# Residual sums into the tile's other buffer, and the first pair's tiles spread over more groups of the MLP stage

## The chip, the cores and the metric

One Trainium2 chip, one core. The time is the device time of one execution in microseconds (us); the median of three runs of the kernel before is 3148.65 us (3146.72 to 3151.5).

## The reference

For x of 2 x 4096 x 512 (8192 tokens, model width 512), all in float32:

```
xn = layernorm(x)
a  = xn + ssm_scan(rmsnorm(xn, scale1))                # a diagonal state space model over the sequence
h  = gelu(rmsnorm(a, scale2) @ w1 + b1) @ w2 + b2      # 512 -> 2048 -> 512, exact gelu
f  = fp4_linear(silu(fp4_linear(xn, w_gate)) * fp4_linear(xn, w_up), w_down)   # 512 -> 1408 -> 512, blockwise FP4
out = x + (a + h) + f
```

The change touches only how the tiles of `h` are prepared: for each tile of 128 tokens, `a` (called x1), the sum of squares of x1, the normalized rows, and the residual sum `z + b2 + x1`, where z holds x + f.

## The kernel before, in words

The work is cut into 64 tiles of 128 tokens. Every float32 operand of a matmul is split into a high and a low half (fp32r), and a product takes three passes (`PASSES`). Five programs, one per engine, are written out in full; each engine takes its instructions in this written order, and semaphores tie them together. SP (the sync engine) issues all DMAs, in its own order, and waits where its program waits.

Until about 1725 us the kernel computes the FP4 layers of all tiles and the state space scan. r_Z holds x + f per tile, r_Y the scan's result.

Then comes the MLP stage (1725 to 1990 us), with `NB1 = 2` blocks of four tiles, tiles 0 to 7. Its loop is `for n in range(2, 16 * NB1 + 2)` in each program. In group n PE does `mlp1(n)` (first layer, feature block n % 16, twelve matmuls into one bank) and `mlp2(n - 2)` (second layer, twelve). `mlp1(n)` needs the GELU of group n - 2 (its bank is free then), and in the first block the low half of weight set n; `mlp2(n - 2)` needs the split GELU of its group. `mlp1(16)` needs all of tiles 4 to 7. At n = 17 DVE writes block 0's results, and SP stores them. The programs of DVE, ACT and POOL in group n are, in order:
- DVE: `w_low(n + 2)` (low halves of a weight set, while n + 2 < 16), `gelu_parts(n)`, from n = 26 on a turn or low half of the first pair's operands (`conv_turn`, `conv_sums`, `conv_low`), `result` at 17 and 33, then the steps of `mlp_steps(n)`, then those of `early_steps(n)`.
- ACT: `w_high(n + 2)`, `gelu(n)`, the scale of combined weights k (`combine_scale`) and the high half of the k of one group earlier (`combine_high`, one buffer `wh`, which waits for the store of the k before), then the tile steps.
- POOL: `combine_sums`, `combine_low`, then the tile steps.
- SP: the store of the low half, the store of the high half and the load of the combined weights, the tile steps, from n = 18 on one `ring_load` per group, and at n = 29 and 31 `quarters`.

A tile's steps have three parts. Part 0: `tile_add` on DVE (x1 = normalized x + scan result, in `xl`, after the loads of `xl` and `yl`), `tile_square` on ACT (writes its squares to `yl`, which no one reads, and the sum of squares), `tile_z` on POOL (`zl + b2`, then `+ x1`), on SP the load of the next `zl` (tiles below 8). Part 1: `tile_root` on DVE (eleven small steps and the scale of `xl`, which waits for `tile_z`), and on SP the stores and loads that follow. Part 2, tiles 4 to 7 only: DVE turns the tile, ACT writes its high half to `hT`, DVE the low half, and SP issues the loads of the tile after next (`pre_load(t + 2)`), which use the same slot and wait for DVE's turn (`s_hs`). `xl` and `yl` exist twice (slot 0 and slot 1), `zl` once.

`mlp_steps(n)` says in which group each part of tiles 4 to 7 runs (L165); within a group, part 2 stands ahead of 0 and 1. `early_steps(n)` (L197) says so for o = 8 to 15, the tiles of the first pair of blocks; part 1 stands ahead of part 0. For these SP does, in part 1 of o:

```
store_sum(o)      # r_Q <- residual sum, after s_zx1
store_normed(o)   # r_N <- xl, after the scale
z_load(o + 1)
pre_load(o + 2)   # for o = 14 and 15: quarters(0, 0) and quarters(0, 1)
```

`quarters` loads the normalized rows back in quarters for the transposition by `conv_turn`. After the loop come seven pairs of blocks (`unit` and `rest`), with products from combined weights that the ring brings in, and the tiles of the next pair prepared by the same functions, one per unit.

Of the kernel before, what the change touches and what calls it, by code (L numbers as in the profile page):

```python
# [39 lines left out]

NB1 = 2
PAIRS = (NT // 4 - NB1) // 2
OLD = 4 * NB1
# [4 lines left out]
WSC0, WSUM0, WAH0, WAL0, HT0 = 4 * NST, 4 * NST, 3, 4, 11  # L48
RING_0, OQ_0, ZQ_0, WT_0, Q_0, WA_0, WB_0, QO_0 = 32, 16, 8 * NT, 16, 16, 16, 16, 16
QUADS = ((0, 1), (2, 3), (4, 0), (1, 2))  # L50
# [114 lines left out]
def mlp_steps(n):  # L165

    b, f = n // 16, n % 16
    if b + 1 >= NB1:
        return []
    at = [(2, 3, 6), (4, 5, 8), (8, 9, 12), (10, 11, 14)]  # L170
    return [(4 * (b + 1) + j, part) for part in (2, 0, 1) for j in range(4) if at[j][part] == f]
# [25 lines left out]
def early_steps(n):  # L197

    return [(OLD + r, part) for part in (1, 0) for r in range(8) if 14 + 3 * r // 2 + part == n]

# [8 lines left out]
def build(nc, x, A, B, C, Dv, sc1, sc2, w1, b1, w2, b2, wg, wu, wd, cst, out):  # L209
# [15 lines left out]
    with ExitStack() as ctx:  # L225
# [308 lines left out]
        def sync_program(e):  # L534
# [148 lines left out]
            def pre_load(o):  # L683
# [14 lines left out]
                e.dma_start(xl[k][:], xt[t]).then_inc(d_xl[o % 2], 16)  # L698
                if p is not None:
                    e.wait_ge(s_sq, p + 1)  # L700
                for i in range(2):
                    e.dma_start(yl[k][:].rearrange("p (g i k) -> p g i k", i=2, k=16)[:, :, i],
                                bass.AP(r_Y.tensor, (64 * i + t) * P * 16, [[16, P], [P * P * 16, 16], [1, 16]])
                                ).then_inc(d_yl[o % 2], 16)

            def z_load(o):
                if o >= NT:
                    return
                t = tile_of(o)
# [15 lines left out]
            def quarters(c, i):  # L725
# [43 lines left out]
            def ring_load(q):  # L769
                if q >= 56 * PAIRS:  # L770
                    return
                if q < 14:
                    e.wait_ge(s_w1, 17 + q)
                    e.wait_ge(d_wa, WA_0 + 16 * 4)
# [4 lines left out]
            def residual_in(c, i):  # L779
                r = 2 * (i % 4) + i // 4  # L780
                if i % 4 < 2 and 2 * c + i // 4 == 0:
                    e.wait_ge(s_w1, 32)
                elif i % 4 >= 2 and i < 4:
# [161 lines left out]
            for n in range(2, 16 * NB1 + 2):  # L945
# [15 lines left out]
                for o, part in early_steps(n):  # L961
                    if part == 1:
# [5 lines left out]
                        else:  # L968
                            quarters(0, o - OLD - 6)
                if 18 <= n < 32:  # L970
                    ring_load(n - 18)
                if n in (29, 31):
                    quarters(0, (n - 25) // 2)
            pre_load(OLD + 8)
# [297 lines left out]
        def vector_program(e):  # L1272
# [374 lines left out]
            def second_part(c, i):  # L1647
# [9 lines left out]
                elif q == 2:  # L1657
                    e.wait_ge(d_oo[6], 16)
                    e.wait_ge(d_oo[7], 16)
                e.tensor_copy(second_high(q), gelued(half, f)).then_inc(s_gh, 1)  # L1660

            def unit(c, u):
# [8 lines left out]
                if g == 0:  # L1671
                    e.wait_ge(d_oo[4], 16)
                e.tensor_tensor(u2[:], bank[5][:], s1[:], ALU.add).then_inc(s_add, 1)
                e.wait_ge(s_p, 7 * g + 3)
                e.wait_ge(s_add, 5 * g + 1)
                if g == 0:
                    e.wait_ge(d_oo[5], 16)
                e.tensor_tensor(u3[:], bank[6][:], u2[:], ALU.add).then_inc(s_add, 1)  # L1678
# [76 lines left out]
            for n in range(2, 16 * NB1 + 2):  # L1755
# [5 lines left out]
                if n < 16 * NB1:  # L1761
                    gelu_parts(n)
                if n >= 26 and n % 2 == 0:
                    conv_turn(0, n // 2 - 13)
                    conv_sums(0, n // 2 - 13)
                elif n >= 27:
                    conv_low(0, n // 2 - 13)
                if (n - 2) % 16 == 15:
# [11 lines left out]
        def scalar_program(e):  # L1780
# [215 lines left out]
            def conv_high(c, i, x):  # L1996
# [3 lines left out]
                if c == 0 and i == 0 and x == 0:  # L2000
                    e.wait_ge(s_w1, 24)
                    e.wait_ge(d_wa, WA_0 + 16 * 16)
                    for j in range(2):
                        e.wait_ge(d_wb[j], WB_0 + 16 * 8)
                    for j in range(4):
                        e.wait_ge(d_oo[j], 16)
                elif c and i == 0 and x == 0:
# [69 lines left out]
            for n in range(2, 16 * NB1 + 2):  # L2077
# [13 lines left out]
                if n >= 26 and n % 2 == 0:  # L2091
                    for x in range(5):
                        conv_high(0, n // 2 - 13, x)
            for c in range(PAIRS):
# [5 lines left out]
        def gpsimd_program(e):  # L2100
# [92 lines left out]
            def tile_z(t):  # L2193
                b, j = t // 4, t % 4
                zz = zx[b % 2][:, j] if t < OLD else zl[:]
                e.wait_ge(d_zl, 16 * (t + 1))
                if t == 0:
                    e.wait_ge(d_cv[0], 16)
                if t == 4:
                    e.wait_ge(s_dn, NW)  # L2200
# [72 lines left out]
            for n in range(2, 16 * NB1 + 2):  # L2273
# [9 lines left out]
                if n >= 27 and n % 2:  # L2283
                    conv_low(0, n // 2 - 13)
            for c in range(PAIRS):
# [65 lines left out]
```

## Time and profile before

| | us |
|---|---|
| median of three runs | 3148.65 |
| the profiled execution | 3141.06 |
| its span | 3139.3 |
| PE busy | 3003.8 (96%) |
| DVE busy | 2186.5 (70%) |
| POOL busy | 1601.4 (51%) |
| ACT busy | 1157.2 (37%) |

A busy share is that of all matmuls; in a row of the timeline the second number is the time from the first start to the last end of the merged instructions, and the bracket holds the idle time of the engine just before, with what ended it. SPq is the queue of DMA issues of SP; an issue's time is not the transfer's. PEclk is the granted clock of TensorE in parts of full speed (2.4 GHz).

### The profile page before, as it was taken

Reading aid. Unit: us, or ns where it says so; the run is one execution under the profiler, and the core shown is the slowest. Engines: PE = TensorE matmul, PEld = TensorE weight load, DVE = VectorE, ACT = ScalarE, POOL = GpSimd, SP = SyncE. Lnnn points to the kernel's source line nnn. Section 1 sums busy time; section 2 is a strip of 40 time slices with the busy share of each in tenths; the row PEclk is TensorE's granted clock in tenths of the full one; section 3 lists DMA queues with packets and bytes.
Section 4 is the critical chain, followed back from the end, with each engine's and each line's share of the span. In section 5 each row is a group of like instructions: output and inputs, shape, how many; then the busy total and the mean of one; then the engine's idle time right before and its main releaser. Section 6 shows DMA issues by size and latency. Waiting matters only on the chain. (4 is left out here: it accounts for less than half of the span.)

```text
span 3139.3 us, 44091 instructions
## 1 busy us (share of the span) xinstructions
PE 3003.8 (96%) x14525; PEld 2417.3 (77%) x14525; DVE 2186.5 (70%) x4455; ACT 1157.2 (37%) x1930; POOL 1601.4 (51%) x1457
## 2 busy tenths in 40 slices
PE   5799999999999999999999877999999999999999
PEld 3678788888877777777777765788888888878887
DVE  8798898987787766767777766656565656565622
ACT  5345655645443443333323432222222222222220
POOL 7556666655555555555454554344454535453413
PEclk9999999999999999999999998999999999999999
DMA  4133334357666666666633788877767677768541
GB/s 127 45 89 96 113 113 117 97 136 188 184 174 168 164 161 175 158 159 167 170 87 94 198 211 200 198 209 174 201 179 209 172 202 182 207 166 215 143 131 47
DMA packets 975794, 488.77 MB, mean 156 GB/s; under 512 B 689232, under 2 KB 817488, under 8 KB 973008
## 3 DMA queue, kind: packets, MB, share of 16 engines
q1 hardware_dynamic: 975568, 485.96, 58.6%
q8 instruction: 118, 1.93, 0.3%
q14 instruction: 108, 0.88, 0.1%
HBM read 346.84 MB, written 138.97 MB: 155 GB/s over the span
## 5 line engine op out<-in xcount | busy, mean ns | idle before, releaser
L1029 PE MATMUL bank<-XT,Wu 128*128 128x512 f32 (+1 forms) x2148 | 515.6, 389 | 15.9 <-DVE sg L1314 15.7
L1029 PE MATMUL bank<-XT,Wg 128*128 128x512 f32 (+1 forms) x2148 | 522.8, 392 | 7.3 <-DVE Wd L1381 7.3
L1051 PE MATMUL bank<-Wd,HT 128*128 128x512 f32 x2112 | 515.6, 393 | 6.6 <-POOL HT L2130 5.3
L2122 POOL TENSOR_TENSOR qa<-qb,qs 128x512 f32<-128x512 f32 (+2 forms) x277 | 308.4, 1114 | 342.5 <-DVE qb L1374 340.1
L1029 PEld LDWEIGHTS bank<-XT,Wu 128*128 128x128 f32 x2148 | 401.0, 190 | 106.6 <-issue 25.7
L1051 PEld LDWEIGHTS bank<-Wd,HT 128*128 128x128 f32 x2112 | 391.7, 188 | 106.1 <-issue 15.4
L1029 PEld LDWEIGHTS bank<-XT,Wg 128*128 128x128 f32 x2148 | 397.3, 189 | 96.0 <-DVE Wd L1381 9.4
L1225 PE MATMUL bank<-Wp,G 128*128 128x512 f32 x1800 | 456.4, 390 | 3.3 <-POOL G L2243 3.3
L1203 PE MATMUL bank<-HC,Wp 128*128 128x512 f32 x1680 | 423.5, 390 | 2.8 <-POOL WH L2236 2.8
L1225 PEld LDWEIGHTS bank<-Wp,G 128*128 128x128 f32 x1800 | 336.7, 188 | 77.4 <-POOL G L2243 7.9
L1203 PEld LDWEIGHTS bank<-HC,Wp 128*128 128x128 f32 x1680 | 316.4, 188 | 69.2 <-POOL WH L2236 3.2
L2130 POOL TENSOR_TENSOR HT<-qb,HT 128x512 fp32r<-128x512 f32 (+1 forms) x179 | 229.9, 1284 | 241.5 <-ACT HT L1816 241.3
L2116 POOL TENSOR_TENSOR qa<-qa,qs 128x512 f32<-128x512 f32 (+1 forms) x243 | 263.0, 1082 | 109.0 <-DVE qs L1354 109.0
L1816 ACT ACTIVATE HT<-qb 128x512 fp32r<-128x512 f32 (+1 forms) x179 | 112.2, 627 | 413.8 <-DVE qb L1328 413.7
L2243 POOL TENSOR_TENSOR G<-gf,G 128x512 fp32r<-128x512 f32 x75 | 103.5, 1379 | 303.6 <-DVE G L1660 303.6
L1225 PE MATMUL bank<-Wp,G2x 128*128 128x512 f32 x888 | 229.0, 390 | 2.0 <-POOL G2x L2243 2.0
L1366 DVE SCALAR_TENSOR_TENSOR qa<-qb,qa 128x512 f32<-128x512 f32 (+2 forms) x149 | 120.7, 810 | 140.9 <-ACT qb L1788 140.6
L1225 PEld LDWEIGHTS bank<-Wp,G2x 128*128 128x128 f32 x888 | 166.1, 188 | 38.5 <-POOL G2x L2243 4.2
L1823 ACT ACTIVATE sg<-bank 128x512 f32<-128x512 f32 (+1 forms) x179 | 105.6, 590 | 203.2 <-PE bank L1029 199.8
L1203 PE MATMUL bank<-WH,Wp 128*128 128x512 f32 x672 | 172.5, 393 | 3.7 <-DVE u L1678 2.4
L1349 DVE TENSOR_REDUCE qs<-qa 128x32 f32<-128x512 f32 (+1 forms) x243 | 165.1, 680 | 8.3
L1328 DVE STREAM_TRANSPOSE qb<-qa 128x512 f32<-128x512 f32 (+1 forms) x179 | 124.9, 698 | 55.6 <-POOL qa L2122 55.6
(199 smaller groups left out, 4420.2 us busy)
## 6 DMA issues: line engine op xcount, KB each, us to landing
Wp<-r_A SPq DMA_DIRECT2D x392, 256.0 KB, 3.3
px<-in_L_attn_x_dram SPq DMA_DIRECT2D x128, 256.0 KB, 3.2
xin<-in_L_attn_x_dram SPq DMA_DIRECT2D x128, 256.0 KB, 3.3
sT<-r_K SPq DMA_DIRECT2D x128, 256.0 KB, 4.1
r_Z<-xin SPq DMA_DIRECT2D x64, 256.0 KB, 2.4
r_U<-ub SPq DMA_DIRECT2D x16, 1024.0 KB, 6.7
sU<-r_U SPq DMA_DIRECT2D x32, 512.0 KB, 4.9
r_Y<-sY SPq DMA_DIRECT2D x16, 1024.0 KB, 5.3
```

Of the source, the lines that this page charges most:

```text
L1029: ins = e.matmul(bk[:, 0:n], W[wh][:, k, :], inputs(xh, w, k), start=(k == 0 and p_ == 0), stop=(k == KD - 1 and p_ == 2))
L1051: ins = e.matmul(DNB[t % 4][:], HT[hh][:, w % 2, a * P:(a + 1) * P], Wd[wh][:, f, :], start=(w == first(n) and p_ == 0), stop=(w == last(n ...
L1203: ins = e.matmul(bank[bk][:], ring(q)[:, 256 * wh_ + P * kt:256 * wh_ + P * kt + P], combined(b, xh)[:, kt], start=(k in OPENS and kt == 0 ...
L1225: ins = e.matmul(bank[4 * half + j][:], (second_high(q), second_low(q))[gh][:, j * P:(j + 1) * P], Wp[f][wh_][:, 1, :], start=(f == 0 and ...
L1328: e.transpose(qb[:, m % 2, 0:n], qa[:, m % 4, 0:n]).then_inc(s_t2, 1)
L1349: e.tensor_reduce(s_, blk(job_in(m)), AX, ALU.max, apply_absolute_value=True).then_inc(s_mx, 1)
L1366: e.scalar_tensor_tensor(Aa, Bb, FLOOR, Aa, ALU.max, ALU.add).then_inc(s_t, 1)
L1816: e.activation(HT[0][:, w % 2, 0:n], qb[:, m % 2, 0:n], ACT.Copy).then_inc(s_hh, 1)
L1823: e.activation(sg[:, 0:n], GB[:, 0:n], ACT.Silu).then_inc(s_sg, 1)
L2116: e.tensor_tensor(blk(qa[:, m % 4, 0:n]), blk(job_in(m)), bc(qs[:, m % 4, 1, 0:n // 16], n // 16), ALU.mult).then_inc(s_pa, 1)
L2122: e.tensor_tensor(blk(qa[:, m % 4, 0:n]), blk(qb[:, m % 2, 0:n]), bc(qs[:, m % 4, 0, 0:n // 16], n // 16), ALU.mult).then_inc(s_ph, 1)
L2130: e.tensor_tensor(lo, qb[:, m % 2, 0:n], hi.bitcast(F32), ALU.subtract).then_inc(s_hl, 1)
```

## The change

`tile_z` writes the residual sum of tiles 8 and up to `yl` of the tile's slot instead of `zl`, once ACT's Square has gone over it; SP stores it from there. So `zl` is free for the next load as soon as POOL has read it (`s_zx1`), and the load of the next `yl` in that slot, and the first two `quarters`, wait for the store of the sum (`d_qo`) instead of the Square. Tiles 6 and 7 run two groups sooner, and the first pair's tiles begin at group 12 rather than 14, one every 7/4 groups instead of 3/2:

| | before | after |
|---|---|---|
| tile 6: parts 0, 1, 2 in group | 8, 9, 12 | 6, 7, 10 |
| tile 7 | 10, 11, 14 | 8, 9, 12 |
| o = 8 to 15, part 0 | 14 15 17 18 20 21 23 24 | 12 13 15 17 19 20 22 24 |
| part 1 | one later each | one later each |

The remaining edits write constants with `LASTB = 16 * (NB1 - 1)` or `OLD`; with `NB1 = 2` they have the same values, and a new wait in `tile_z` for `8 <= t < OLD` is never reached (`OLD` is 8).

```diff
+LASTB = 16 * (NB1 - 1)
...
-    at = [(2, 3, 6), (4, 5, 8), (8, 9, 12), (10, 11, 14)]
+    at = [(2, 3, 6), (4, 5, 8), (8, 9, 12), (10, 11, 14)] if b + 2 < NB1 else [(2, 3, 6), (4, 5, 8), (6, 7, 10), (8, 9, 12)]
...
-    return [(OLD + r, part) for part in (1, 0) for r in range(8) if 14 + 3 * r // 2 + part == n]
+    return [(OLD + r, part) for part in (1, 0) for r in range(8) if LASTB - 4 + 7 * r // 4 + part == n]
...
                 e.dma_start(xl[k][:], xt[t]).then_inc(d_xl[o % 2], 16)
-                if p is not None:
+                if p is not None and p < OLD:
                     e.wait_ge(s_sq, p + 1)
+                elif p is not None:
+                    e.wait_ge(d_qo, QO_0 + 16 * (p - OLD + 1))
...
                 if o > OLD:
-                    e.wait_ge(d_qo, QO_0 + 16 * (o - OLD))
+                    e.wait_ge(s_zx1, o)
                 e.dma_start(zl[:], r_Z[t]).then_inc(d_zl, 16)
...
-                e.dma_start(r_Q[tile_of(o)], zl[:]).then_inc(d_qo, 16)
+                e.dma_start(r_Q[tile_of(o)], yl[slot(o)][:]).then_inc(d_qo, 16)
...
-                    e.wait_ge(s_sq, o + 1)
+                    e.wait_ge(d_qo, QO_0 + 16 * (o - OLD + 1))
...
-                zz = zx[b % 2][:, j] if t < OLD else zl[:]
+                zz, to = (zx[b % 2][:, j], zx[b % 2][:, j]) if t < OLD else (zl[:], yl[slot(t)][:])
...
-                e.tensor_tensor(zz, zz, xl[slot(t)][:], ALU.add).then_inc(s_zx1, 1)
+                if t >= OLD:
+                    e.wait_ge(s_sq, t + 1)
+                e.tensor_tensor(to, zz, xl[slot(t)][:], ALU.add).then_inc(s_zx1, 1)
```

## Rows read from the trace of the kernel before

**Rows 1.** Windows: span, busy (x instructions) of PE, PEld, DVE, ACT, POOL, clock, DMA, GB/s
```profile
1725.70:1839.40 113.70, 93.08 (x380) 73.48 (x378) 82.39 (x151) 50.45 (x99) 59.30 (x59) 0.93 0.75 198
1839.40:1989.80 150.40, 118.28 (x444) 93.11 (x444) 96.65 (x209) 38.69 (x78) 64.06 (x63) 0.89 0.80 195
1989.80:3139.30 1149.50, 1140.13 (x5004) 937.03 (x5004) 644.00 (x1430) 275.23 (x492) 493.66 (x366) 1.00 0.67 176
```

**Rows 2.** Waits of PE, 1725 to 2000: total us, times, longest
```profile
PE bank L1152 <- ACT gf L1976: 15.8, 5, 4.9
PE bank L1168 <- DVE G L1588: 11.1, 4, 5.3
PE bank L1152 <- DVE hT L1573: 9.0, 1, 9.0
```

**Rows 3.** Timeline of PE: start, us, instructions, idle time before
```profile
1784.66 3.01 PE L1152 MATMUL bank<-hT,Wp 128*128 128x512 f32 x12
...
1798.07 4.60 PE L1152 MATMUL bank<-hT,Wp 128*128 128x512 f32 x12 [2.24 <-ACT gf L1976]
...
1813.56 3.01 PE L1152 MATMUL bank<-hT,Wp 128*128 128x512 f32 x12 [2.56 <-ACT gf L1976]
...
1839.43 4.60 PE L1152 MATMUL bank<-hT,Wp 128*128 128x512 f32 x12 [9.05 <-DVE hT L1573]
...
1867.13 2.88 PE L1168 MATMUL bank<-Wp,G 128*128 128x512 f32 x12
...
1888.32 5.49 PE L1168 MATMUL bank<-Wp,G 128*128 128x512 f32 x12 [4.71 <-DVE G L1588]
```

**Rows 4.** Timeline of DVE, groups 6 to 9
```profile
1782.79 1.13 DVE L1573 SCALAR_TENSOR_TENSOR hT<-bank,vec,hT 128x128 fp32r<-128x128 f32 x4 [1.21 <-ACT hT L1959]
...
1793.98 1.66 DVE L1546 TENSOR_TENSOR xl<-xl,yl 128x512 f32<-128x512 f32 x1
1796.96 1.29 DVE L1537 TENSOR_TENSOR Wp<-Wr,Wp 128x512 fp32r<-128x512 f32 x2 [1.31 <-ACT Wp L1935]
```

**Rows 5.** Line 702 from 1785 to 1789: tile 6's yl loads, from issue to landing
```profile
L702 SPq DMA_DIRECT2D yl<-r_Y x2: 499/1700/2902, 1785.5 to 1786.0; - x2
...
DMA to landing us min/median/max: 5.7/6.3/6.8
```

**Rows 6.** Timeline of SP: tile 5's store and its four loads
```profile
1776.52 0.33 SPq L839 DMA_DIRECT2D r_H<-xl  x1
1778.79 2.60 SPq L842 DMA_DIRECT2D xl<-r_H  x4
```

**Rows 7.** Timeline of ACT ahead of tile 7's high half
```profile
1836.13 1.06 ACT L1994 ACTIVATE wh<-wt 128x1024 fp32r<-128x1024 f32 x1 [5.73 <-DMA r_A<-wh]
```

**Rows 8.** Timeline of SP: the first and the last of eight sum stores
```profile
1844.60 0.70 SPq L719 DMA_DIRECT2D r_Q<-zl  x1
...
1940.04 0.58 SPq L719 DMA_DIRECT2D r_Q<-zl  x1
```

**Rows 9.** Waits of SP between these two
```profile
SPq L714 <- DMA r_Q<-zl: 14.9, 7, 2.6
SPq L754 <- POOL wl L2227: 9.3, 3, 4.3
SPq L763 <- ACT wh L1994: 5.2, 2, 4.6
```

**Rows 10.** Waits of DVE, 1860 to 1945
```profile
DVE xl L1558 <- POOL zl L2207: 16.5, 3, 7.1
```

**Rows 11.** Timelines of POOL, ACT, DVE in the pairs' first unit
```profile
1985.02 1.27 POOL L2207 TENSOR_TENSOR zl<-zl,xl 128x512 f32<-128x512 f32 x1 [9.01 <-DVE xl L1546]
...
1984.98 0.63 ACT L1941 ACTIVATE yl<-xl 128x512 f32<-128x512 f32 x1 [6.67 <-DVE xl L1546]
1985.51 0.19 ACT L1941 ACTIVATION_READ_ACCUMULATOR yl<-xl 128x1 f32 x1
...
1988.35 0.49 DVE L1558 TENSOR_SCALAR xl<-xl,rs 128x512 f32<-128x512 f32 x1
```

More of the change, by code:

```diff
@@ L48 @@
 WSC0, WSUM0, WAH0, WAL0, HT0 = 4 * NST, 4 * NST, 3, 4, 11
-RING_0, OQ_0, ZQ_0, WT_0, Q_0, WA_0, WB_0, QO_0 = 32, 16, 8 * NT, 16, 16, 16, 16, 16
+RING_0, OQ_0, ZQ_0, WT_0, Q_0, WA_0, WB_0, QO_0 = 32, 2 * OLD, 8 * NT, 16, 16, 16, 16, 16
 QUADS = ((0, 1), (2, 3), (4, 0), (1, 2))
@@ L772, in ring_load @@
                 if q < 14:
-                    e.wait_ge(s_w1, 17 + q)
+                    e.wait_ge(s_w1, LASTB + 1 + q)
                     e.wait_ge(d_wa, WA_0 + 16 * 4)
@@ L781, in residual_in @@
                 if i % 4 < 2 and 2 * c + i // 4 == 0:
-                    e.wait_ge(s_w1, 32)
+                    e.wait_ge(s_w1, 16 * NB1)
                 elif i % 4 >= 2 and i < 4:
@@ L969, in sync_program @@
                             quarters(0, o - OLD - 6)
[L970 to L973, printed above, removed]
+                if LASTB + 2 <= n < 16 * NB1:
+                    ring_load(n - LASTB - 2)
+                if n - LASTB in (13, 15):
+                    quarters(0, (n - LASTB - 9) // 2)
             pre_load(OLD + 8)
@@ L1657, in second_part @@
                 elif q == 2:
-                    e.wait_ge(d_oo[6], 16)
-                    e.wait_ge(d_oo[7], 16)
+                    e.wait_ge(d_oo[6], 2 * OLD)
+                    e.wait_ge(d_oo[7], 2 * OLD)
                 e.tensor_copy(second_high(q), gelued(half, f)).then_inc(s_gh, 1)
@@ L1671, in unit @@
                 if g == 0:
-                    e.wait_ge(d_oo[4], 16)
+                    e.wait_ge(d_oo[4], 2 * OLD)
                 e.tensor_tensor(u2[:], bank[5][:], s1[:], ALU.add).then_inc(s_add, 1)
@@ L1676, in unit @@
                 if g == 0:
-                    e.wait_ge(d_oo[5], 16)
+                    e.wait_ge(d_oo[5], 2 * OLD)
                 e.tensor_tensor(u3[:], bank[6][:], u2[:], ALU.add).then_inc(s_add, 1)
@@ L1762, in vector_program @@
                     gelu_parts(n)
[L1763 to L1767, printed above, removed]
+                i = (n - LASTB) // 2 - 5
+                if i >= 0 and n % 2 == 0:
+                    conv_turn(0, i)
+                    conv_sums(0, i)
+                elif i >= 0:
+                    conv_low(0, i)
                 if (n - 2) % 16 == 15:
@@ L2000, in conv_high @@
                 if c == 0 and i == 0 and x == 0:
-                    e.wait_ge(s_w1, 24)
+                    e.wait_ge(s_w1, LASTB + 8)
                     e.wait_ge(d_wa, WA_0 + 16 * 16)
@@ L2005, in conv_high @@
                     for j in range(4):
-                        e.wait_ge(d_oo[j], 16)
+                        e.wait_ge(d_oo[j], 2 * OLD)
                 elif c and i == 0 and x == 0:
@@ L2090, in scalar_program @@
                         tile_square(o)
-                if n >= 26 and n % 2 == 0:
+                i = (n - LASTB) // 2 - 5
+                if i >= 0 and n % 2 == 0:
                     for x in range(5):
-                        conv_high(0, n // 2 - 13, x)
+                        conv_high(0, i, x)
             for c in range(PAIRS):
@@ L2198, in tile_z @@
                     e.wait_ge(d_cv[0], 16)
-                if t == 4:
+                if 8 <= t < OLD:
+                    e.wait_ge(d_oo[t % 8], 16 * (t // 8))
+                elif t == 4:
                     e.wait_ge(s_dn, NW)
@@ L2282, in gpsimd_program @@
                         tile_z(o)
-                if n >= 27 and n % 2:
-                    conv_low(0, n // 2 - 13)
+                if n >= LASTB + 11 and n % 2:
+                    conv_low(0, (n - LASTB) // 2 - 5)
             for c in range(PAIRS):
```

## The prediction

> **What bounds the kernel now.** I read the page's busy shares, then windows, waits and timelines. The windows [rows 1] show where PE has anything to give. From 1989.80 to the end (seven pairs of token blocks) it is busy 1140.13 of 1149.50 us, so what happens upstream of it can give back 9.4 us at most there. In the stage that the diff reschedules, PE is idle 20.6 us between 1725.70 and 1839.40 (113.70 less 93.08) and 32.1 us from there to 1989.80, at a mean granted clock of 0.93 and 0.89. The list of waits [rows 2] names ACT and DVE, never a transfer. PE's timeline [rows 3] adds the second half of each price: twelve matmuls take 2.88 us at the full clock (2.4 GHz), and 4.60, 4.60 and 5.49 us, partly at 1.2 GHz, where they follow an idle time of 2.24, 9.05 or 4.71 us. A stall costs its idle time and some 1.7 to 2.6 us more.
>
> A group n of this stage is one first-layer and one second-layer set of twelve matmuls, 5.44 us of PE. In the timeline, group 9 begins at 1784.66, group 11 at 1798.07, group 13 at 1813.56, group 16 at 1839.43 [rows 3].
>
> **Part 1: tiles 6 and 7 are added two groups sooner** (8 to 6, 10 to 8). Their loads do not move with them. Tile 6 uses the slot of tile 4, so SP issues its loads once DVE has turned tile 4, and that is in group 6 too, just ahead of the add in DVE's own program. Two groups lay between load and use; now none. Tile 7 stands to tile 5 in the same way in group 8.
> Tile 6: DVE ends tile 4's low half at 1782.79 + 1.13 = 1783.9 [rows 4]. SP issues yl's two transfers at 1785.5 and 1786.0, and they land 5.7 and 6.8 us later, at 1792.3 to 1792.8 [rows 5]. With its 0.7 us the add ends at about 1793.2 instead of 1784.6: DVE waits 8.5 us. Queued behind it: on DVE the low halves of group 9's weights and group 7's GELU split; on ACT, whose Square waits for that add, the weights' high halves and a GELU; on POOL the residual sum and the combined weights. In the rows of before such an add ends at 1793.98 + 1.66 = 1795.6, the weights' low halves begin at 1796.96, and PE goes on at 1798.07, 2.4 us after the add [rows 3, 4]. So group 9 begins at 1793.2 + 2.4 = 1795.6, not 1784.66: +10.9 us.
> The Trainium skill (DMA: Bandwidth & Descriptors, "Anatomy of one DMA") gives about 2.0 us as a transfer's fixed part; by that alone, an estimate, yl would have landed at 1788 and DVE's wait be 4 us. The 5.7 to 6.8 us of this trace disagree and are what the sum uses.
> Tile 7: tile 6's normalized rows are ready 6.5 us after its add (an estimate: 1.3 of wait and 1.29 for the weights [rows 4], some 3.4 for the split and the root's short steps, 0.49 for the scale [rows 11]), 1799.7. SP stores them, goes on 2.27 us later and issues four loads in 2.60 us [rows 6]: 1804.6. Another 1.0 us for the combined weights; tile 7's second yl at 1806.9, landed 5.7 to 6.3 us later, 1812.9. DVE has been done with tile 5's turn since 1805 and waits 7.6 us. Add, then 2.4 us: group 11 at 1815.9 in place of 1798.07, **+17.8 us**. Bounds for both tiles: +10 if yl lands within the 2.27 us that the r_H store takes [rows 6], +22 if both take 6.8 and SP is late by 2 us each time.
>
> **Part 2: what comes back until group 16.** Tile 7's add no longer stands before group 13, where PE was idle 2.56 us [rows 3]. Tile 7's last part leaves group 14 for 12. Before, PE stood 9.05 us for it ahead of group 16: ACT had it queued behind the high half of the combined weights, which waited 5.73 us for a store of r_A to land [rows 7]; with the slow set (4.60 for 2.88) 10.8 us. ACT will still wait for that store, but then only the GELUs of groups 14 and 15 are behind it, which PE needs one and two groups later. So 13.4 us come back. I charge 2 us for a new wait, GELU 14 behind tile 9's Square. Group 16 is then **about 6 us** late, at 1845.5. Bounds: +3 with fewer new waits, +17 if the whole wait returns under the name of a GELU.
>
> **Part 3: tiles 8 to 15, one per 7/4 groups.** SP sets the pace here. It issues the first of eight sum stores at 1844.60, the last at 1940.04: 95.4 us, 13.6 per tile [rows 8], while 1.5 groups of PE are 8.2 us. In this stretch SP waits 14.9 us for these stores to land, 9.3 for POOL, 5.2 for ACT [rows 9]. The first of these stays: the load of zl no longer waits for the store, but the load of yl behind it does, and the one of xl between them waits for the r_N store issued next to it. What is new is that zl comes about 2 us sooner (14.9 over 7 waits), and that each tile has more room. DVE sat 16.5 us in three waits for POOL's sum [rows 10]: tiles 11, 13 and 15, which followed their neighbours by one group; now only 13 does. PE's largest stalls on "DVE G" (4.71 us before one set [rows 3], 11.1 us in all [rows 2]) came of them.
> The sum. SP's floor for the seven steps is 95.4 - 9.3 - 5.2 and some 5 us of smaller waits, 76 us; the ceiling is 95.4. I take 84: zl frees POOL sooner, which pays half of the 19 us, but the one wh buffer still admits one store at a time. The first sum store moves from group 15 to 13, 10.9 us sooner by PE's count, and it is later by the +17.8 of Part 1 less the two groups' part of what Part 2 gives back (2.6) and less the small waits that DVE's delay swallows (some 4): about 1845, as before. The last is at 1845 + 84 = 1929, in place of 1940.04: **-11 us**. What is late next is that same store: the combined weights' last low half and the quarter loads of the first pair stand beside it in SP's program, as before, and the conversion waits for them; so the first pair's product moves by the same -11 us.
>
> **Part 4: the same code in the pairs.** 48 tiles there write their sum to yl after ACT's Square. Cost 0, hidden by DVE's root: in the first pair POOL's add starts at 1985.02, the Square at 1984.98, and with its read it is done at 1985.7; the add would end at 1985.7 + 1.27 = 1987.0, and DVE needs it for the scale at 1988.35 [rows 11]. Were this cover gone, each tile would hold DVE by under 1 us, 43 us in all, of which PE would show what exceeds its slack. Bounds: -3 (part of the 9.4 us of idle time goes) to +10. The yl load's new wait is for a store issued three steps earlier.
>
> **Sum.** +6 at group 16, then -17 to the last sum store: -11 us on the profiled execution's 3141.06 (span 3139.3), 3130. The median of the runs, 3148.65, is 7.6 us above that execution; by that measure the forecast is 3148.65 - 11, **3137.5 us**, its own range 3127 to 3144.
>
> **Rivals.**
> (a) The two waits for loads are not paid back; slower. ACT and POOL wait in order with the add, so the combined weights, which held ACT in [rows 7], slip with it. With group 16 at +17 the first sum store is at about 1856, and at a pace of 90 us the last is at 1946, +6; at 95.4, +11: 3155 to 3160. It decides once group 16's delay over the forecast exceeds the pace's gain of 11 us. Against it: Part 2's idle time was measured, and its cause is moved. Chance 0.23.
> (b) SP's pace stays 95.4 us, the waits for POOL and ACT turning up elsewhere since the DMA engines are 0.80 busy [rows 1]; zl and yl have merely changed places. The last sum store is then at 1940.5: 0 us, 3148.5. Chance 0.19.
> (c) SP reaches its floor of 76 us and group 16 is at +3: 1842 + 76 = 1918, -22 us, 3127. For it: all three waits of DVE have lost their cause. Chance 0.15.
> The forecast keeps 0.43.
>
> **Numbers.** Under 0.2% (6.3 us) can't be told from no change. Faster by more: (c) and most of the forecast's, 0.55. Same: (b) and an edge of its neighbours, 0.20. Slower: (a) and Part 4's upper end, 0.25. The range runs from 3124, (c) with Part 4's 3 us, to 3158, within (a).
>
> **What would show it.** Part 1: waits of DVE on "DMA yl<-r_Y" of 7 to 10 us in groups 6 and 8, and group 11 at about 1816. Part 2: no wait "DVE hT"; group 16 near 1845. Part 3: SP's wait moved from the zl load to those behind it, DVE's waits on "POOL zl" under 6 us in sum, 84 us between first and last sum store. Part 4: PE's idle time in the pairs within 3 us of 9.4. Wrong, if DVE waits for yl under 3 us (then faster than (c)) or over 12 each, or if PE loses time in the pairs.

## The result and the profile after

| | before | after |
|---|---|---|
| median, 9 runs each | 3151.12 us | 3158.12 us |
| lowest to highest | 3146.72 to 3152.49 | 3154.39 to 3162.09 |
| profiled execution, span | 3141.06, 3139.3 | 3156.87, 3155.1 |

The ratio after/before is 1.0026, 95% interval [1.0016, 1.0037]: the change costs 7 us by the medians (5 to 12 by the interval). The forecast of -11 us was wrong in its sign; +7 lies in the range of rival (a), +6 to +11.

The trace behind the rows of before is of an execution some 10 us faster than that kernel's median. A second trace of the same kernel, taken with the experiments ("b2" below), spans 3148.3 us; the comparisons from here on are with it, except where rows are named. Two traces of one kernel thus differ: by 1.4 us at groups 9 and 16, 3.0 us at the last sum store and 1.8 us in the time between first and last sum store (95.4 in [rows 8], 97.2 in b2). Differences of that size between single traces say nothing. Against b2 the changed kernel spans 6.8 us more, as the medians do.

What PE waited for between 1725 and 2010 us in the changed kernel (total, times, longest):

```profile
PE bank L1155 <- ACT gf L1980: 37.7, 7, 10.2
PE bank L1155 <- DVE Wp L1540: 11.1, 4, 4.0
PE bank L1171 <- DVE zx L1602: 5.9, 1, 5.9
PE bank L1206 <- DVE u L1681: 4.1, 1, 4.1
PE bank L1171 <- DVE G L1591: 2.1, 4, 0.8
```

The same view of b2:

```profile
PE bank L1152 <- ACT gf L1976: 15.3, 5, 5.1
PE bank L1168 <- DVE G L1588: 12.2, 4, 5.8
PE bank L1152 <- DVE hT L1573: 8.5, 1, 8.5
PE bank L1152 <- DVE Wp L1537: 6.6, 3, 3.4
PE bank L1168 <- DVE zx L1599: 5.4, 1, 5.4
```

Two waits went, as intended: "hT" altogether (8.5) and most of "G" (12.2 to 2.1), 18.6 us. Two grew: the GELU's by 22.4 us and the weights' ("Wp") by 4.5. PE's timeline in the changed kernel says where; compare [rows 3]:

```profile
1796.97 5.49 PE L1155 MATMUL bank<-hT,Wp 128*128 128x512 f32 x12 [10.16 <-ACT gf L1980]
...
1819.61 4.69 PE L1155 MATMUL bank<-hT,Wp 128*128 128x512 f32 x12 [8.59 <-ACT gf L1980]
...
1834.39 3.00 PE L1155 MATMUL bank<-hT,Wp 128*128 128x512 f32 x12 [0.65 <-DVE Wp L1540]
...
1849.01 3.00 PE L1155 MATMUL bank<-hT,Wp 128*128 128x512 f32 x12 [3.47 <-DVE Wp L1540]
...
1858.47 5.46 PE L1155 MATMUL bank<-hT,Wp 128*128 128x512 f32 x12 [3.74 <-ACT gf L1980]
```

These are groups 9, 11, 13, 15 and 16. DVE's timeline before groups 9 and 11 (small steps left out) shows one cause, the wait for the loads of tiles 6 and 7 (6.6 us in group 6, 5.1 in group 8; the runs below put the rest beside it); the rows of before are [rows 4]:

```profile
1785.58 1.12 DVE L1576 SCALAR_TENSOR_TENSOR hT<-bank,vec,hT 128x128 fp32r<-128x128 f32 x4 [1.21 <-ACT hT L1963]
1791.21 0.55 DVE L1545 TENSOR_SCALAR xl<-xl,mv,rst 128x512 f32<-128x512 f32 x1 [4.51 <-DMA xl<-in_L_attn_x_dram]
1793.86 0.69 DVE L1549 TENSOR_TENSOR xl<-xl,yl 128x512 f32<-128x512 f32 x1 [2.09 <-DMA yl<-r_Y]
1795.86 1.29 DVE L1540 TENSOR_TENSOR Wp<-Wr,Wp 128x512 fp32r<-128x512 f32 x2 [1.31 <-ACT Wp L1939]
...
1814.10 0.55 DVE L1545 TENSOR_SCALAR xl<-xl,mv,rst 128x512 f32<-128x512 f32 x1 [3.27 <-DMA xl<-in_L_attn_x_dram]
1816.49 0.69 DVE L1549 TENSOR_TENSOR xl<-xl,yl 128x512 f32<-128x512 f32 x1 [1.85 <-DMA yl<-r_Y]
```

And ACT's timeline shows how it reaches PE: after 9 us of waiting for that add comes the Square, then the weights' high halves, then the GELU that frees PE's bank:

```profile
1794.58 0.63 ACT L1945 ACTIVATE yl<-xl 128x512 f32<-128x512 f32 x1 [9.04 <-DVE xl L1549]
1795.12 0.19 ACT L1945 ACTIVATION_READ_ACCUMULATOR yl<-xl 128x1 f32 x1
1795.21 1.13 ACT L1939 ACTIVATE Wp<-Wr 128x512 fp32r<-128x512 f32 x2
1796.25 0.67 ACT L1980 ACTIVATE gf<-bank,vec 128x512 f32<-128x512 f32 x1
```

SP's timeline shows tile 6's store and its four loads; compare [rows 6] for tile 5:

```profile
1802.33 0.33 SPq L842 DMA_DIRECT2D r_H<-xl  x1
1804.35 3.59 SPq L845 DMA_DIRECT2D xl<-r_H  x4
```

It has the first and last sum store 96.5 us apart, about as far as before [rows 8]. Between the first two rows SP waits 3.3 us for POOL's low half of combined weights, right ahead of the first sum store:

```profile
1850.33 0.68 SPq L766 DMA_DIRECT2D r_A<-wh  x1
1854.34 0.37 SPq L757 DMA_DIRECT2D wt<-in_L_attn_w_dram  x1
1854.75 0.47 SPq L722 DMA_DIRECT2D r_Q<-yl  x1
...
1951.21 0.91 SPq L722 DMA_DIRECT2D r_Q<-yl  x1
```

### The profile page after: what moved, and what is told of

Same layout as the page of the kernel before. It is cut to its first block and busy times, and to the rows that moved or that the text cites. A ratio compares the mean times of both kernels' runs of the same rounds, so it can differ in the third digit from the quotient of the medians.

```text
span 3155.1 us, 44091 instructions
## 1 busy us (share of the span) xinstructions
PE 3005.8 (95%) x14525; PEld 2418.0 (77%) x14525; DVE 2192.7 (69%) x4455; ACT 1156.5 (37%) x1930; POOL 1601.6 (51%) x1457
```

## The experiments

Each is read at the same seven places. Groups are those of PE's first-layer sets; "sums" are the starts of SP's first and eighth sum store, "steps" the time between them; "product" is the start of the first pair's first product. us from the span's start, from one profiled execution each; the ratio is that of the timed runs to the kernel before on the same chip. The runs that leave out loads or read other rows (no_loads67, plain_yl, no_loads_pair, no_wt_loads, both_short, all_short) compute something else and only serve to time the rest.

```
                 gr. 9    gr. 11   gr. 13   gr. 16   first sum  last sum  steps  product  ratio [95%]
b2 (before)      1786.07  1799.62  1815.32  1840.88  1845.89    1943.07    97.2  1977.59  0.9999 [0.9990, 1.0008]
after            1796.97  1819.61  1834.39  1858.47  1854.75    1951.21    96.5  1985.45  1.0026 [1.0016, 1.0037]
yl_only          1787.48  1799.93  1815.47  1841.99  1847.69    1944.34    96.7  1977.86  1.0003 [0.9994, 1.0012]
sched_only       1797.13  1819.66  1834.45  1857.47  1853.95    1954.70   100.8  1988.74  1.0042 [1.0030, 1.0055]
tiles67_only     1797.07  1819.82  1834.60  1851.04  1862.25    1959.12    96.9  1993.76  1.0054 [1.0041, 1.0066]
turn_sooner      1786.84  1800.35  1815.87  1839.20  1848.91    1947.19    98.3  1981.80  1.0011 [1.0002, 1.0020]
one_sooner       1786.70  1805.36  1822.64  1848.91  1852.79    1948.19    95.4  1982.52  1.0019 [1.0010, 1.0028]
no_loads67       1792.37  1809.84  1824.61  1847.95  1844.23    1939.29    95.1  1973.51  0.9990 [0.9981, 0.9999]
plain_yl         1792.72  1813.71  1828.47  1851.90  1848.18    1940.30    92.1  1974.52  0.9979 [0.9969, 0.9988]
act_high         1788.57  1801.49  1817.26  1840.71  1846.11    1939.65    93.5  1973.55  0.9984 [0.9975, 0.9993]
act_high_after   1795.21  1816.40  1831.17  1854.01  1850.29    1943.82    93.5  1977.51  1.0010 [1.0001, 1.0019]
late_preload     1796.47  1819.07  1833.86  1857.45  1853.92    1958.35   104.4  1993.32  1.0056 [1.0042, 1.0070]
act_late_yl      1787.13  1800.05  1815.69  1840.94  1846.19    1938.43    92.2  1971.84  0.9978 [0.9969, 0.9987]
act_ring_yl      1786.87  1799.79  1815.42  1838.96  1845.12    1936.56    91.4  1969.04  0.9975 [0.9964, 0.9985]
no_loads_pair    1798.01  1820.99  1835.79  1859.59  1855.88    1946.44    90.6  1981.59  1.0017 [1.0007, 1.0027]
no_wt_loads      1796.81  1819.36  1834.13  1857.59  1849.81    1942.86    93.1  1977.85  1.0006 [0.9996, 1.0016]
both_short       1796.40  1818.76  1833.53  1857.02  1849.25    1940.24    91.0  1974.92  0.9997 [0.9987, 1.0007]
short_low        1798.19  1821.51  1836.27  1859.83  1856.10    1950.74    94.6  1984.86  1.0019 [1.0007, 1.0030]
all_short        1796.72  1819.33  1834.10  1857.73  1849.94    1927.10    77.2  1962.04  0.9952 [0.9933, 0.9972]
```

One thing holds in every row: the product begins 32 to 35 us after the last sum store (34.5 in b2, 34.2 after). The end of the stage follows the last sum store, not PE's place in group 16.

### The parts of the change, one by one

**b2**, the kernel before.

> The kernel before, unchanged, to have its trace and its time from the same chip as the others. The trace of before that the forecast used was 8 to 10 us below that kernel's median. If that was chance, this trace spans about 3149 us and the extra lies outside the MLP stage (1725 to 1990); PE's idle time in the pairs is then the number to compare the changed kernel with: under 8 us there if the changed kernel's pairs are really slower (it had 10.5 us of named waits there against 6.6), 10 us or more if not.

It spans 3148.3 us. PE's waits in the pairs (from 2010 us on) are 5.4, 3.2 and 0.8 us on G, G2x and GX, 9.4 in sum; in the changed kernel 4.7, 3.5 and 0.8, 9.0. The pairs cost nothing. The trace of before was a short one: 6.1 us of these waits, and its first product at 1975.33, 2.3 us ahead of b2's; so not all of the difference lies outside the MLP stage.

**yl_only**, the sum in yl, all tiles in their groups of before:

```diff
-    at = ... if b + 2 < NB1 else [(2, 3, 6), (4, 5, 8), (6, 7, 10), (8, 9, 12)]
-    ... if LASTB - 4 + 7 * r // 4 + part == n]
+    at = [(2, 3, 6), (4, 5, 8), (8, 9, 12), (10, 11, 14)]
+    ... if 14 + 3 * r // 2 + part == n]
```

> Only the sum in yl; the tiles stay in their groups of before. Theory 1 (the loss is the loads of tiles 6 and 7, the buffer gives a little by an earlier zl): -1 to -5 us against before, no wait of DVE on yl loads, DVE's waits on POOL's sum fall from 16.5 to 8-12 us. Theory 2 (POOL's add behind ACT's Square holds the split of the second part in the pairs): PE's waits on POOL G in the pairs rise by 3 to 4 us, and the whole is 0 to +3.

1.0003: nothing. DVE's three waits for POOL's sum fell to 14.0 us only, where theory 1 wanted 8 to 12. PE's waits on POOL in the pairs are 11.0 us in sum against b2's 9.4, less than theory 2's 3 to 4 us more.

**sched_only**, the complement: the new groups, the old buffer.

> Only the new groups (tiles 6 and 7 two sooner, the pair's tiles from 12, one per 7/4); the sum stays in zl and its load waits for the store as before. Theory 1: group 11 about 20 us late, group 16 about 18 us late, the last sum store 10 to 14 us late, in all +6 to +12 us; the pairs as in before. Theory 2 puts 3 to 4 us of the changed kernel's loss into the buffer: this one is then 3 to 4 us faster than the changed kernel in the pairs.

Group 11 is 20.0 us late, group 16 16.6, the last sum store 11.6, as expected; the whole, +13 us, is a little over the +12. With the load of zl behind the store again, the new order takes 100.8 us for its steps. So the two parts interact: the buffer is worth nothing in the old order, and 4 us of steps and 5 us of the whole in the new one. In the pairs this run waits as long as the changed kernel (8.8 us against 9.0): theory 2 fell.

**tiles67_only**, only tiles 6 and 7 moved, one line:

```diff
-    at = [(2, 3, 6), (4, 5, 8), (8, 9, 12), (10, 11, 14)]
+    at = [(2, 3, 6), (4, 5, 8), (6, 7, 10), (8, 9, 12)]
```

> Only tiles 6 and 7 two groups sooner; tiles 8 and up start in group 14 as before, sum in zl. Tells the price of the loads from what stands ahead of group 16. Theory 1a (the forecast's Part 2 was right for tiles 6 and 7, and what spoiled it is that tiles 8 and 9 came into groups 12 and 13): group 11 at +18 to +20 us, group 16 at +6 to +9, and from there the old stage; in all +4 to +8. Theory 1b (the delay is not paid back at all, whatever stands in groups 12 and 13): group 16 at +17 or more, in all +12 or more.

Both theories fell, each in half. Group 16 is 10.2 us late, so half of the delay is paid back in PE's own count (1a, a little more than its 6 to 9). The whole is 16 to 17 us slower all the same (1b), because SP comes to the first sum store 16.4 us late and stays that late.

**turn_sooner**, from the kernel before, only the last parts a group earlier (`(8, 9, 11), (10, 11, 13)`).

> The kernel before, with only the last parts (turn, hT) of tiles 6 and 7 one group sooner (12 to 11, 14 to 13), their adds where they were. Takes away what PE waited 9 us for ahead of group 16 without asking for a load at the moment it is issued. If PE's time lost in block 0 counted by itself: -8 to -10 us. If the end follows the sum stores (as in the four runs so far, where group 16 was 10 to 18 us late and the end followed the first sum store): the first sum store moves by 2 to 5 us at most, as tile 8 is still added in group 14, and the whole by the same -2 to -5 us.

The 8.5 us before group 16 are gone from PE's waits, but from group 13 to group 15 PE takes 6.3 us more, so group 16 is only 1.7 us sooner. The first sum store comes 3 us later. SP's timeline shows a reason, though 3 us is no more than two traces of one kernel can differ: tile 8's loads now stand ahead of tile 7's store, SP issues the next load of wt at 1828.90 instead of 1825.26, and ACT's longest wait for wt is 11.2 us instead of 3.0. Removing the longest stall of the block by itself gave no gain (1.0011, its interval just above 1).

**one_sooner**: adds in 7 and 9, turns in 11 and 13, `13 + 11 * r // 7` for the pair.

> The changed kernel with tiles 6 and 7 only one group sooner than before (adds in 7 and 9, turns in 11 and 13), the pair's tiles in 13 14 16 17 19 20 22 24. Loads are now issued one group ahead of their use. Theory 1 (half of the 20 us up to group 11 is the loads, half that the add stands in the group of a turn, as the run without loads showed): both go, group 11 within 4 us of before; first sum store 1846 to 1850; in all -2 to +4 us against before. Rival (the stage's crowding does not care for one group): group 11 at +8 or more, in all +5 or more.

Group 9 is on time, group 11 5.7 us late: between the theory's 4 and the rival's 8. The first sum store is 6.9 us late. One group between issue and use removes most of Part 1's price, and the whole is +5 to +6 us, at the lower end of the rival's.

**no_loads67**, the changed kernel without the loads of xl and yl of tiles 6 and 7:

```diff
                 t, p, k = tile_of(o), before(o), slot(o)
+                if o in (6, 7):
+                    return
...
-                e.wait_ge(d_xl[o % 2], 16 * (o // 2 + 1))
+                e.wait_ge(d_xl[o % 2], 16 * (o // 2 + 1 - (o >= 6)))
```

> The changed kernel without the loads of xl and yl of tiles 6 and 7 (they add what lies in the slot; this leaves their input out of the computation, everything else runs). Takes away the wait that the two earlier groups create. Theory 1 (DVE's wait for those loads, and what is queued behind it, is the loss up to group 11): group 11 within 3 us of the kernel before (1799.6), no PE stall of 8 to 10 us before groups 9 and 11; the end then shows what the rest of the new order is worth: first sum store 15 to 19 us sooner than in the changed kernel, in all 12 to 18 us under it, 5 to 10 under before. Rival (the new groups crowd DVE, ACT and POOL whatever the loads do): group 11 stays 8 us or more late, in all under 6 us back.

The end moves less than theory 1 expected: the first sum store comes 10.5 us sooner and not 15 to 19, the whole is 11 us under the changed kernel and not 12 to 18, and 3 under before and not 5 to 10. It is still more than the loss itself: without the loads of these two tiles the changed kernel is a little faster than before. Group 11 is between the two: 10.2 us late instead of 20.0. PE still idles 3.5 us before each of groups 9 and 11, and twelve matmuls take 5.49 us after the first of these:

```profile
1792.37 5.49 PE L1157 MATMUL bank<-hT,Wp 128*128 128x512 f32 x12 [3.47 <-ACT gf L1982]
```

So the loads are about half of Part 1's loss (9.8 of 20.0 us). The other half remains without them. one_sooner, where the add is out of the turn's group as well, has 5.7 us of it left; that the add, its Square and the weights crowd the group of a turn is the reading that fits both runs, not one that was tested alone.

### What makes the pace of the eight tiles

**plain_yl**: yl from contiguous rows of r_Z, for every tile, those of the pairs too.

> The changed kernel with yl loaded from contiguous rows of another array (1 KB pieces instead of 64 B; the scan's result is left out of the sums). Two transfers as before, but each is quick to issue (0.3 to 0.5 us instead of 1.1 to 3) and lands in about 3 us. Theory SP (SP's own time sets the pace of the tiles 8 to 15, 96.6 us here and 97.3 before): the seven steps between sum stores take 8 to 14 us less, 83 to 89 us, and groups 9 and 11 start 2 to 4 us sooner each; in all 12 to 20 us under the changed kernel. Rival (the combined weights' chain ACT - store - landing - ACT sets the pace): the seven steps take 93 us or more; in all 4 to 6 us.

Groups 9 and 11 came 4.3 and 5.9 us sooner, the steps took 4.4 us less, not 8 to 14. The theory "SP's own time" got a third to a half of what it asked there. The whole is 15 us under the changed kernel (0.9979 against 1.0026), inside its 12 to 20: 6.6 us from the earlier first sum store, 4.4 from the steps, the rest behind the first product. So the changed kernel with quick yl loads beats the kernel before by 6 us; it is the largest gain of any single relief.

**act_high** (on before) and **act_high_after** (on after): ACT issues the high half's store.

```diff
                 e.activation(wh[:], wt[:, k % 2], ACT.Copy).then_inc(s_wah, 1)
+                e.wait_ge(s_wah, WAH0 + k + 1)
+                e.dma_start(bass.AP(r_A.tensor, ...), wh[:].bitcast(F32)).then_inc(d_wa, 16)
...
-                    store_sums_high(k)
```

> The kernel before, with ACT issuing the store of the combined weights' high half itself, right after it has written it. SP loses 16 issues (0.6 to 1.3 us each) and its waits for ACT (5.5 us of the stretch between the first and the last sum store). Theory SP: that stretch 97.3 falls to 82 to 90 us, in all -6 to -14 us. Rival (the chain through the one wh buffer): the store leaves sooner, so this gives too, but then the waits of ACT on 'DMA r_A<-wh' vanish and SP's issues of wt follow ACT at once; if neither is the limit (transfers at 0.82 busy), the stretch stays above 94 us and the whole within 3 us.

> The changed kernel with ACT issuing the high half's store itself. Before, this gave 5 us (3.7 us less between the sum stores, group 16 as early). If the parts add up: -5 to -7 us against the changed kernel, +0 to +3 against before. If the chain through wh is what the new order overloads (ACT waits 26.3 us for r_A to land here, 8.7 before): -10 to -16 us against the changed kernel, the seven steps at 82 to 88 us.

Both took 3 to 4 us off the steps, 5 to 6 us off the whole (0.9984, and 1.0010 where the change alone has 1.0026). On the kernel before this lies between the two theories; on the changed one the parts add up. The wait of ACT on the store's landing fell to 3 us in both, from 8.7 and 26.3. That the larger wait brought no more says that it alone was not what held the pace.

**late_preload**: SP's loads for tile o + 2 one group later.

> The changed kernel with SP's two loads for tile o + 2 issued one group later, behind that group's combined weights, so that SP does not stand still while the stores just issued land (16.1 + 2.2 us between the first and the last sum store). Theory SP (SP's own time, waits for its stores included, makes the pace): the seven steps take 8 to 16 us less than 96.5, in all -8 to -14 us against the changed kernel. Rival (pace set by the loop of combined weights through ACT, POOL and the landing of r_A, each 11 to 12 us per set): SP's wait turns up at POOL's wl or at ACT's wh, the steps still take 93 us or more, in all within 4 us.

SP's wait on its own stores fell from 18.3 to 5.9 us, and the steps took 8 us more: SP waited 24.7 us for POOL's wl instead of 9.4, and DVE 14.1 us for the later loads instead of 1.3. The whole is 9 us over the changed kernel. Moving the loads behind the combined weights freed no time: in sum SP waited longer than before, and DVE came to need the loads.

**act_late_yl** and **act_ring_yl**, two candidates in the groups of before.

> The groups of before, the sum in yl, the high half's store on ACT, the loads for tile o + 2 one group later. A candidate to beat both kernels. Theory SP: 18 us of SP's standing still and 16 issues gone: -12 to -20 us against before, seven steps at 78 to 86 us. Rival: as much as the ACT store alone gave, -4 to -7 us.

> The groups of before, the sum in yl, and ACT issues both the high half's stores and the ring loads of groups 18 to 31. A candidate to beat both kernels, beside the one that has the later loads. If SP's issues count (14 of 0.5 to 1.4 us): 3 to 6 us more than the 6 us of the ACT store alone, -8 to -12 us against before; if not, -4 to -7 us.

3140.18 and 3139.04 us against 3147.8: 0.9978 and 0.9975. Both beat the kernel before, by 7 to 9 us, and the changed one by twice that. Their intervals overlap, so neither is the better one. What they gave is what the ACT store alone was to give and a little more; the 12 to 20 us of the theory of SP's time did not come, and the ring loads on ACT brought at most 3 us more than the stores alone (0.9984).

**no_loads_pair**, **no_wt_loads**, **both_short**: the changed kernel without the loads of xl and yl of tiles 10 to 15; without the wt loads from the ninth set on; without both.

> The changed kernel without the loads of xl and yl for tiles 10 to 15 (their input is left out; DVE waits for the stores from the slot itself). The two slots make a loop: stores of tile o land, loads for o + 2 are issued and land, add, root, scale, stores. Slot theory (this loop makes the pace of 96.5 us): the seven steps take 75 to 85 us. Chain theory (the combined weights' loop, 11 to 12 us a set, makes it): 90 us or more. SP loses 12 issues with it, 2.3 us per tile, which plain_yl showed to be worth 4 us.

> The changed kernel without the loads of wt for the combined weights from the ninth on (scaled and summed as before from what lies there, ACT waits for POOL instead of for the load). Takes out of the combined weights' loop the load and SP's wait for POOL in front of it (9.4 us in the stretch). Slot theory: the seven steps take 88 us or more. Chain theory: 75 to 85 us.

> Both at once, in the changed kernel. If one of the two loops made the pace, this adds under 4 us to what the better one of them gives. If they take turns (each released by the other through the written order of the engines), each alone gives 3 to 8 us and both together 20 us or more: 65 to 76 us for the seven steps.

Steps of 90.6, 93.1 and 91.0 us (96.5): 5.9, 3.4 and 5.5 us off. Neither theory of one loop holds, and "both by turns" (20 us) doesn't either. The steps alone mislead here, as no_wt_loads also brings the first sum store 4.9 us sooner (the wait for POOL's low half ahead of it goes). At the last sum store, which the end follows, the three runs give 4.8, 8.4 and 11.0 us: the two reliefs nearly add up, and so do the timed runs (3, 6 and 9 us under the changed kernel). The windows of the stretch (span, busy of PE, PEld, DVE, ACT, POOL, clock, DMA, GB/s) say what was left. The changed kernel:

```profile
1854.75:1951.21 96.46, 77.08 (x300) 61.53 (x301) 66.89 (x132) 26.25 (x49) 52.82 (x50) 0.89 0.88 225
```

and with both reliefs:

```profile
1849.25:1940.24 90.99, 77.84 (x308) 62.10 (x307) 77.08 (x140) 26.15 (x49) 55.10 (x54) 0.89 0.63 189
```

DVE's busy time is 10 us more, for eight more instructions (140 for 132), and DVE is now as busy as PE: 77.1 us of 91.0, with 9.6 us of waits. Its timeline there shows single instructions at 2.6 us:

```profile
1913.28 2.59 DVE L1567 TENSOR_SCALAR xl<-xl,rs 128x512 f32<-128x512 f32 x1
...
1916.86 2.67 DVE L1551 TENSOR_SCALAR xl<-xl,mv,rst 128x512 f32<-128x512 f32 x1
...
1927.05 2.63 DVE L1567 TENSOR_SCALAR xl<-xl,rs 128x512 f32<-128x512 f32 x1
```

and POOL's timeline has its longest one at each of these places:

```profile
1913.19 2.40 POOL L2244 TENSOR_TENSOR wl<-wt,wh 128x1024 fp32r<-128x1024 f32 x1
1916.84 2.40 POOL L2244 TENSOR_TENSOR wl<-wt,wh 128x1024 fp32r<-128x1024 f32 x1 [1.25 <-ACT wh L2006]
...
1927.00 2.40 POOL L2244 TENSOR_TENSOR wl<-wt,wh 128x1024 fp32r<-128x1024 f32 x1 [1.17 <-ACT wh L2006]
```

**short_low** and **all_short** shorten exactly that instruction, alone and on top of both reliefs:

```diff
-                e.tensor_tensor(wl[k % 2][:], wt[:, k % 2], wh[:].bitcast(F32), ALU.subtract)
+                m = 8 if k < 8 else 1
+                e.tensor_tensor(wl[k % 2][:, 0:m], wt[:, k % 2, 0:m], wh[:, 0:m].bitcast(F32), ALU.subtract)
```

> The changed kernel with POOL's low half of the combined weights, from the ninth set on, on 128 of its 1024 columns (the rest of these low halves is left as it was). DVE's instructions that begin beside POOL's 2.4 us one took 2.3 to 2.7 us instead of 0.5 in the traces, so DVE's busy time of 66.9 us in the stretch may itself be part of the pace. Port theory: DVE busy falls by 8 to 14 us there, the seven steps take 84 to 90 us, in all -6 to -12 us against the changed kernel. Rival (stretching fills DVE's waits for loads and GELUs, of which there are 24 us): DVE's busy time falls, its waits grow by as much, the steps take 94 us or more.

> The same short low half together with both reliefs of before (no loads of xl and yl for tiles 10 to 15, no loads of wt from the ninth set on). With both reliefs the seven steps took 91.0 us, of which DVE was busy 77. Port theory: 70 to 80 us, as now nothing but DVE's own work and PE's 65 us for twelve groups are left. Rival: 86 us or more; then it is the written order of the groups, not a resource, that holds the pace.

Alone it gives 1.8 us of steps, no more than two traces of one kernel differ, and 0.5 us at the last sum store; DVE's busy time falls from 66.9 to 54.3 and its waits grow by 10 us instead, the rival's picture. On top of the other two it gives 13.8 us: 77.2 us for the steps, 0.9952 for the whole. The windows of all_short:

```profile
1849.94:1927.10 77.16, 72.17 (x298) 58.71 (x298) 61.50 (x141) 26.27 (x49) 40.42 (x54) 0.94 0.74 223
```

In the steps the three reliefs alone give 5.9, 3.4 and 1.8 us, the first two together 5.5, all three 19.3; at the last sum store 4.8, 8.4 and 0.5, the first two 11.0, all three 24.1. So the third is hidden behind the loads: nothing by itself, 13 us once they are gone. Whether it is DVE held up beside POOL or POOL's own time is not parted by these runs, as the short low half also takes 14.7 us off POOL's busy time (55.10 to 40.42); that DVE was the fuller of the two speaks for the first. With all three gone PE is the limit: of the 77.2 us it is busy 72.2 and waits 5.0, its first-layer sets start 5.44 us apart from 1880.50 to 1929.46, and its waits are these:

```profile
PE bank L1173 <- DVE zx L1608: 2.9, 1, 2.9
PE bank L1157 <- ACT gf L1986: 2.1, 1, 2.1
```

## Why the prediction was wrong, step by step

**Part 1** (tiles 6 and 7) held in its mechanism, and came nearer in its number than it had earned. Group 9: +10.9 us forecast, +10.9 measured against b2. Group 11: +17.8 forecast, +20.0 measured. DVE was to wait 8.5 and 7.6 us; it waited 6.6 in group 6 (4.5 for xl, 2.1 for yl) and 5.1 in group 8 (3.3 and 1.9). That group 9 agrees to a tenth is luck: the wait was 1.9 us shorter, and against b2 the turn ahead of it ended 1.4 us later (1786.70 instead of 1785.33) and the normalization added 0.55. The term was priced as load time alone; no_loads67 shows that about half of it stays without the loads. The 2.2 us more at group 11 come from SP: tile 6's rows went to their store at 1802.33 where the forecast had 1799.7, the four loads took 3.59 us instead of 2.60, and tile 7's last yl load was issued at 1811.0 instead of 1806.9. It then landed in 5.4 us. One of the signs misled: under 3 us of wait for yl was to mean a faster kernel. The waits for yl were 2.1 and 1.9 us because xl's came first, and the kernel was slower. The 2.0 us that Part 1 sets beside these landings, from the Trainium skill (DMA: Bandwidth & Descriptors, "Anatomy of one DMA"), are stated there for transfers of the GpSimd path; SP issued these.

**Part 2** failed in its size. 13.4 us were to come back and 2 be charged. What was to go did go: no "hT" wait, no stall before group 13 worth a us. But group 16 was 17.6 us late, not 6. tiles67_only, without tiles 8 and 9 in groups 12 and 13, had 10.2: 9.8 us came back of the 20.0. Bringing tiles 8 and up forward cost 6.4 us (sched_only, which differs from it in that alone; 7.4 in the changed kernel), as the 3.47 and 3.74 us before groups 15 and 16 show, where the forecast charged 2. So its miss of 11 us at group 16 is 2 from Part 1, 4 that did not come back, and 5 for these tiles.

**Part 3** is the step that failed and turned the sign, in both of its terms: the start of the eight tiles and their pace.

The start of the eight tiles was to move by +0.3 us (10.9 sooner for two groups, 17.8 later, 2.6 and 4 taken off) and moved by +8.9. tiles67_only and sched_only part this. With tiles 6 and 7 alone moved, 20.2 us at group 11 are 16.4 at the first sum store, so 3.8 came off where the forecast took 6.6; its 4 us of swallowed waits had no row behind them. Two groups earlier then brought 8.3 us and not 10.9 (the new buffer added 0.8 to that in the changed kernel), because SP comes to the first sum store behind the combined weights, and these slipped with the add, as rival (a) said: the last thing ahead of it is SP's wait of 3.3 us for POOL's low half, and no_wt_loads, which takes that wait away, has the store 4.9 us sooner.

The pace was to be 84 us and was 96.5, against 97.2 in b2. The 84 was a value between 95.4 and a floor of 76, and the floor came from taking SP's waits for POOL and ACT off SP's 95.4 us; half of the difference, as the text argues, would have been 85.7. What was to shrink did shrink: SP's waits in the stretch went from 34.0 to 28.7 us, DVE's for POOL's sum from 16.7 to 6.3. Nothing was gained. A wait of a queue was taken for time on the path, and late_preload, plain_yl and the reliefs each bring a part at most, as other work is about as long. A second possible reason stands in the table of the change: tile 15's part 1 is in group 25 in both orders. Starting two groups sooner puts two more groups of work between the two stores, and in the windows of the stretch PE is busy 77.1 us where b2 has 73.2, DVE 66.9 where b2 has 63.2. The forecast did not price this work. That it is what holds the pace is not shown.

Of the 19 us between forecast and measurement at the last sum store, the start has 8.6 and the pace 10.7: either term alone, put right, would have left a forecast of about no change, and only both give the sign. The outcome is rival (a) in its second form, group 16 at +17 and the pace unchanged, which put +11 us there; against b2 it was +8.1 at the last sum store, +7.9 at the product, +7 in the medians.

**Part 4** held: the pairs' waits are 9.0 us against 9.4.

The conversion beside the last sum store also held: 32 to 35 us from that store to the first product in all nineteen traces.

What stays open: how the loads of the slots, the combined weights and DVE's work hand the wait to each other within a group, and what of the hidden 13 us is DVE's and what POOL's. So it is shown that the changed kernel loses by a later start of the eight tiles at an unchanged pace, and that leaving out the loads of tiles 6 and 7 is enough to undo it; which work sets the pace is shown only in part.

## What to carry to other kernels

Before an add or a multiply is moved ahead in an in-order program, look where its load is issued: if that hangs on an event in the same stretch, the move buys a stall (here 6.6 and 5.1 us of DVE, 20 us at PE with what else stood in the group), and every engine that waits in order hands it on. Find the event that the end follows (here the last of eight stores, 32 to 35 us ahead of the next stage in every run) and price the change there, not at the engine that is busiest. And the waits on one queue are no stock to draw on: relieve one path at a time, and then two and three together, before a gain is promised, and read the gain at the event that the end follows, not only in a difference of two events that can both move.

## What the runs showed of the hardware

A long instruction of POOL with two inputs held up DVE's instruction beside it to its end. In the changed kernel POOL's 128x1024 subtraction ran from 1907.71 to 1910.05; DVE's add of 128x512, which takes 0.69 us by itself, began at 1908.06 and took 2.53:

```profile
1908.06 2.53 DVE L1549 TENSOR_TENSOR xl<-xl,yl 128x512 f32<-128x512 f32 x1 [1.16 <-DMA yl<-r_Y]
```

```profile
1907.71 2.34 POOL L2236 TENSOR_TENSOR wl<-wt,wh 128x1024 fp32r<-128x1024 f32 x1
```

The Trainium skill (SBUF — State Buffer, "Who interferes with whom") says that a DVE instruction with two SBUF inputs, or in a two-port mode, shares a port pair with GpSimd and that whichever starts first keeps it to its end. The traces agree: DVE's add ended 0.54 us after POOL's subtraction, and with that subtraction cut to 128 columns DVE's busy time in the stretch fell from 66.9 to 54.3 us.

What a yl load costs went with its form more than with the stage it was in. Between 1780 and 1945 us the yl loads of the changed kernel, in pieces of 64 bytes, held SP for 0.37 to 3.08 us each (median 1.07) and landed 4.3 to 6.1 us after issue (median 4.8). In contiguous rows of 1 KB (plain_yl, same stretch) they held SP for 0.34 to 0.49 us and landed after 2.5 to 4.4 (median 3.2). In b2's pairs, where PE hardly waits and the DMA engines are busy 0.67 of the time, the 64-byte loads still landed after 4.2 to 7.1 us (median 4.9). The rows are of another array as well, so the array is not parted from the size of the pieces.
